# Window attention, software pipeline of one kernel: transposes three heads behind the scores, weightings on slots 0, 4, 8 and 12

## The chip, the cores and the metric

One Trainium2 chip, one core. The metric is the time of one execution on the device in microseconds; the value given is the median of three runs.

## The reference

Two blocks, each added to its input, on x of 2 x 128 x 128 x 128 (images, channels, rows, columns). The first is a group norm and window attention with relative position bias, the second a group norm and a deformable convolution. The change touches the first only:

```python
xw = x.reshape(B, C, H // ws, ws, W // ws, ws)            # ws = 16, 8 heads of 16 channels
xw = xw.transpose(0, 2, 4, 3, 5, 1).reshape(-1, N, C)     # 128 windows of N = 256 tokens
qkv = xw @ qkv_w.T + qkv_b
attn = jnp.einsum('whnd,whmd->whnm', q, k) * scale
attn = jax.nn.softmax(attn + bias[None], axis=-1)
out = jnp.einsum('whnm,whmd->whnd', attn, v)
out = out @ proj_w.T + proj_b
x = x + out
```

## The kernel before

Attention runs over 64 pairs of windows. A pair has 16 slots, one for each head of its two windows (slots 0 to 7 the first window, 8 to 15 the second). Every engine has its own program, written out by hand slot by slot in a function `pair` (L552 on TensorE, L637 on ScalarE, L749 on VectorE, L362 on SP), and the engines meet only through semaphores, so each engine works strictly in the order of its `pair`. Two pairs make the body of a loop. The first sixteen of the pairs in a loop also take the statistics of the second image on VectorE (L741).

The way of one head: TensorE makes its scores from `stack` into one of two buffers of `s_ps` (L508); they may be overwritten once VectorE is through with the head two before (L505). VectorE adds the bias and takes the row minimum (L716) into `sbias` and `nmax`. ScalarE takes the exponential into `prob` (L623), one of four buffers. TensorE transposes it in four pieces into one of three banks of `pt_ps` (L521); odd heads share one bank. The transposed head is copied to `probT`, even heads by ScalarE (L630), odd ones by VectorE (L725). When four heads are there, TensorE weights the values with them, without dividing (`weigh`, L536), into `o_ps`. The column of ones in `va` gives the row sums along with it. After two weightings, one window, ScalarE copies `o_ps` to `oT` (L635), TensorE transposes that into `x_ps` (`turn_out`, L548), VectorE divides into `on` (`norm`, L731 and L736), and SP stores it to `attended` (L359).

The lags are constants: T_LAG is how many slots after its scores a head is transposed, READ_LAG_A and READ_LAG_V the slot in which ScalarE and VectorE copy it, PV_LAG the slot in which `o_ps` is copied, OUT_AT that of `turn_out` (and the one after it `norm`). Each of these counts from the first head or half of the pair.

In the same slots the next pairs are prepared: TensorE projects q and k of the pair after next in slots 0 and 4 (L486, L490) and v of the next pair in slot 8 (L496), all into `qkv_ps`; ScalarE reads q in slot 1 (L611) and k in slot 4 (L616), VectorE reads v in slot 9 (L703). GpSimd normalises x and splits q and k into three bfloat16 parts (L443 to L452); SP stores these parts (`store_parts`, L340) and loads them again into `stack` as the terms of the score product (`restack`, L354, twelve transfers of 128 KB). All DMAs of attention are issued on SP's queue, in this order: clear a part of far_sums, load a strip of x, restack the next pair, store the second window of the pair before, store the parts, store the first window of this pair.

Of the kernel before, what the change touches and what calls it, by code (L numbers as in the profile page):

```python
# [20 lines left out]
NH = 8  # L21
# [3 lines left out]
PAIRS = B * (H // WS) * (W // WS) // 2  # L25
# [6 lines left out]
SCALE = float(HD) ** -0.5  # L32
T_LAG = 2
READ_LAG_A, READ_LAG_V = 3, 2
PV_LAG = 4
Q_AT, K_AT, V_AT = 0, 4, 8
OUT_AT = 6
AHEAD = 2
# [141 lines left out]
def attention(nc, x, w_qkv, b_qkv, bv_row, rel_rev, attended, rel_rows, parts_dram, info_out, far_sums):  # L180

    with ExitStack() as ctx:
# [15 lines left out]
        gmat = sb("a_gmat", [P, P])  # L199
# [5 lines left out]
        ex = sb("a_ex", [P, 2])  # L205
        gst = sb("a_gst", [P, 2])
# [93 lines left out]
        def _(sp):  # L300
# [61 lines left out]
            def pair(p, par, first=False, left=AHEAD, piece=None):  # L362
# [20 lines left out]
                if not first:  # L383
                    store(p - 1, 1, 1 - par)
                if left == AHEAD:
                    store_parts(p + 2, par)
                store(p, 0, par)

# [12 lines left out]
            pair(PAIRS - 1, 1, left=0)  # L401
            store(PAIRS - 1, 1, 1)
            for par in range(2):
# [66 lines left out]
        def _(pe):  # L470
# [4 lines left out]
            def group_sums(b):  # L475
                pe.wait_ge(gn_step, count(3 * b + 3))
                nc.tensor.matmul(x_ps[:, 0:2], gmat[:], ex[:], start=True, stop=True).then_inc(gn_sum, 1)
                pe.wait_ge(gn_coef, count(9 * b + 1))
# [73 lines left out]
            def pair(p, par, first=False, left=AHEAD):  # L552
                for n in range(SLOTS):
# [3 lines left out]
                    elif not first:  # L557
                        turn(p - 1, n - T_LAG + SLOTS)
                    if n % 4 == 3:
                        if n > 3:  # L560
                            weigh(p, (n - 7) // 4, par)
                        elif not first:
                            weigh(p - 1, 3, 1 - par)
                    if n == OUT_AT and not first:
# [26 lines left out]
            for n in range(SLOTS - T_LAG, SLOTS):  # L591
                turn(PAIRS - 1, n)
            weigh(PAIRS - 1, 3, 1)
            turn_out(2 * PAIRS - 1, 1)
# [79 lines left out]
        def _(dve):  # L674
            def scales(b):
# [5 lines left out]
                dve.wait_ge(gn_sum, count(b + 1))  # L681
                group_scales(nc, dve, x_ps[:, 0:2], gst, gv, gn[:, b, 0:1], gn[:, b, 1:2], gn_coef, 9 * b,
                             gn_ready, 2 * b, gn_root, b)
# [65 lines left out]
            def pair(p, par, first=False, left=AHEAD, piece=None):  # L749
                for n in range(SLOTS):  # L750
# [6 lines left out]
                    if n == OUT_AT + 1 and not first:  # L757
                        norm(2 * p - 1, 1, 1 - par, (p - 1) // 2)
                    if n == NH + OUT_AT + 1:
                        norm(2 * p, 0, par, p // 2)  # L760
                    if n == V_AT + 1 and left >= 1:
# [15 lines left out]
            for m in range(SLOTS - READ_LAG_V, SLOTS):  # L777
                if m % 2 == 1:
                    read_turned(PAIRS - 1, m)
            norm(2 * PAIRS - 1, 1, 1, (PAIRS - 1) // 2)  # L780

# [964 lines left out]
```

## Time and profile before

| | |
|---|---|
| time, median of 3 runs | 3287.48 us (3285.68 to 3289.9) |
| time of the profiled execution | 3290.47 us, span 3288.8 us |
| attention | some 84 to 1527 us of the span |
| busy over the whole span | TensorE 83%, VectorE 83%, ScalarE 56%, GpSimd 35% |
| one steady pair of windows | 22.35 us |

The span covers both blocks; the deformable convolution follows attention and shares no time with it. For a change in attention the shares over the whole span say little, so the rows below are of the steady stretch of attention, in which one pair is like the next. Matmuls are pipelined on TensorE and their ends are modelled, so steps are best read from start to start. A number in square brackets at the end of a timeline row is the time in which the engine stood idle before it, with the instruction that ended the wait.

### The profile page before, as it was taken

The page shows a single profiled execution, that of the slowest core. Times are in us where ns is not written, and L with a number is a line of the kernel's source. Part 1 is how long each engine was busy: PE and PEld are TensorE (multiplying, and loading weights), DVE is VectorE, ACT ScalarE, POOL GpSimd, SP SyncE. Part 2 cuts the span into 40 slices and gives each one's busy share as a digit, 9 for nine tenths or more (in the row PEclk, how much of TensorE's full clock was granted, in tenths as well). Part 3 has the DMA queues.
Part 4 walks back from the last instruction along what each step waited for, and adds up shares of the span by engine and source line. Part 5 has one row for each costly group of instructions (what it writes and reads, how often), then busy time and mean ns, then how long its engine had stood idle before and what let it go on. Part 6 is the DMA issues. An engine that isn't in the chain of part 4 may idle for free.

```text
span 3288.8 us, 77998 instructions
## 1 busy us (share of the span) xinstructions
PE 2733.5 (83%) x22424; PEld 2192.2 (67%) x22424; DVE 2719.8 (83%) x6553; ACT 1828.7 (56%) x3486; POOL 1162.0 (35%) x1557
## 2 busy tenths in 40 slices
PE   1888889999999999995677989998946799999986
PEld 0555555565565556564566888887835688888885
DVE  3888888888888888885667999999945799999996
ACT  0888888888888888884143443333202443334420
POOL 3333233333333333332446231346232441115550
PEclk9999999999999999998988999999978899999998
DMA  7889897888888898895553233333374433333334
GB/s 182 158 157 163 166 148 138 139 140 143 138 141 142 141 139 143 140 144 116 183 158 91 89 99 101 99 103 84 89 261 134 144 101 101 97 101 95 102 89 160
DMA packets 351779, 432.59 MB, mean 132 GB/s; under 512 B 42352, under 2 KB 275200, under 8 KB 346480
## 3 DMA queue, kind: packets, MB, share of 16 engines
q1 hardware_dynamic: 339696, 423.85, 58.5%
q0 software_dynamic: 11904, 6.44, 1.5%
q8 instruction: 102, 1.67, 0.2%
q14 instruction: 77, 0.63, 0.1%
HBM read 283.33 MB, written 147.09 MB: 131 GB/s over the span
## 4 chain that ended last, share of the span: by engine, by line
DVE 24%; issue 10%; DMA 6%; PE 5%; POOL 3%; DVEq 1%; ACT 1%; POOLq 1%; SPq 1%; ACTq 0%
DVE prod L1635 17%; DMA vring<-vals 3%; DVE tt L1619 2%; PE sum_ps L1429 2%; DVE my L1614 2%; DMA vring<-attended 1%; DVE x L1646 1%; PE sum_ps L1384 1%; ACT d_xn L1518 1%; DMA o_sel<-off_out,pos 1%; PE om_ps L1347 1%; POOL gath L1209 1%; PE sum_ps L1333 1%; POOLq L1216 1%; DMA out<-x 0%
## 5 line engine op out<-in xcount | busy, mean ns | idle before, releaser
L623 ACT ACTIVATE prob<-sbias,nmax 128x256 f32<-128x256 f32 x2048 | 903.9, 501 | 203.4 <-DVE nmax L716 201.0
L716 DVE CUSTOM_DVE_ANT_0 sbias<-s_ps,nbias 128x256 f32<-128x256 f32 x2048 | 768.0, 420 | 212.8 <-PE s_ps L508 201.4
L1635 DVE TENSOR_TENSOR prod<-vring,wt_ps 128x1920 f32<-128x1920 f32 (+3 forms) x512 | 898.8, 1815 | 18.8 <-DMA vring<-vals 11.9
L1384 PE MATMUL sum_ps<-d_ident,prod 128*128 128x128 f32 x6400 | 773.0, 279 | 83.5 <-DVE prod L1635 83.4
L1384 PEld LDWEIGHTS sum_ps<-d_ident,prod 128*128 128x128 f32 x6400 | 732.0, 144 | 131.8 <-DVE prod L1635 104.3
L521 PE MATMUL pt_ps<-a_ident,prob 128*128 128x128 f32 x4096 | 645.3, 280 | 140.5 <-ACT prob L623 137.5
L521 PEld LDWEIGHTS pt_ps<-a_ident,prob 128*128 128x128 f32 x4096 | 448.2, 141 | 284.3 <-DVE probT L725 134.3
L1484 ACT ACTIVATE hat<-off,one_col 128x576 f32<-128x576 f32 x128 | 140.7, 1099 | 700.6 <-DVE tt L1619 700.6
L508 PE MATMUL s_ps<-stack 96*128 96x256 bf16 x2048 | 396.6, 275 | 8.1 <-DMA stack<-parts_dram 7.4
L443 POOL CAST parts<-qk 128x1024 bf16<-128x1024 f32 x64 | 66.3, 1036 | 869.9 <-ACT qk L616 869.9
L725 DVE COPY probT<-pt_ps 128x512 f32<-128x512 f32 x512 | 351.9, 687 | 11.9 <-PE pt_ps L521 11.8
L1362 PE MATMUL wt_ps<-tt,d_ident 128*128 128x144 f32 x2304 | 311.1, 291 | 0.0
L508 PEld LDWEIGHTS s_ps<-stack 96*128 96x128 bf16 x2048 | 175.2, 98 | 202.5 <-issue 157.4
L1362 PEld LDWEIGHTS wt_ps<-tt,d_ident 128*128 128x128 f32 x2304 | 306.6, 195 | 1.4
L630 ACT COPY probT<-pt_ps 128x512 f32<-128x512 f32 x512 | 290.2, 567 | 0.0
L536 PE MATMUL o_ps<-probT,va 128*32 128x256 f32 x4096 | 274.1, 385 | 0.9 <-DVE probT L725 0.9
L1224 POOL COPY first_e<-first_at 128x2 f32 x16 | 2.9, 178 | 563.9 <-issue 563.9
L1619 DVE TENSOR_TENSOR tt<-hat,my 128x864 f32<-128x864 f32 x192 | 192.5, 1057 | 8.8
L716 DVE DVE_READ_ACCUMULATOR2_ANT nmax<- 128x1 f32 x2048 | 170.7, 83 | 0.0
L536 PEld LDWEIGHTS o_ps<-probT,va 128*32 128x32 f32 x4096 | 106.9, 109 | 87.9 <-issue 34.1
L1333 PE MATMUL sum_ps<-wproj_sb,vring 128*128 128x128 f32 x512 | 81.9, 321 | 90.4 <-DMA vring<-attended 81.3
L446 POOL TENSOR_TENSOR rest<-qk,parts 128x1024 f32<-128x1024 f32 x64 | 137.0, 2141 | 11.8 <-POOL parts L443 11.8
(170 smaller groups left out, 3382.2 us busy)
## 6 DMA issues: line engine op xcount, KB each, us to landing
stack<-parts_dram SPq DMA_DIRECT2D x768, 128.0 KB, 7.6
vring<-vals SPq DMA_DIRECT2D x270, 320.0 KB
parts_dram<-parts SPq DMA_DIRECT2D x64, 768.0 KB, 6.5
off_out<-off SPq DMA_DIRECT2D x64, 432.0 KB
strips<-x SPq DMA_DIRECT2D x68, 256.0 KB, 3.7
far_sums<-nothing SPq DMA_DIRECT2D x64, 256.0 KB, 2.1
attended<-on SPq DMA_DIRECT2D x256, 64.0 KB
x<-x SPq DMA_DIRECT2D x16, 1024.0 KB, 6.5
```

The costliest lines, as they stand in the source:

```text
L508: mm = nc.tensor.matmul(s_ps[:, n % 2, half, :], stack[:, par, 0, h, at:at + P], stack[:, par, 1, h, w * NT:(w + 1) * NT], start=True, sto ...
L521: mm = nc.tensor.transpose(pt_ps[:, T_BANK[n % 4], kh, half * P:(half + 1) * P], prob[:, n % 4, half, kh * P:(kh + 1) * P], ident[:])
L536: mm = nc.tensor.matmul(o_ps[32 * j:32 * j + VA, t * NT:(t + 1) * NT], va[:, par, 2 * w + kh, 4 * t + j, :], probT[:, (4 * k + j) % 8, kh, ...
L623: ins = nc.scalar.activation(prob[:, n % 4, half, :], sbias[:, n % SBIAS, half, :], ACT.Exp, bias=nmax[:, n % SBIAS, half:half + 1], scale ...
L630: nc.scalar.copy(probT[:, n % 8], pt_ps[:, T_BANK[n % 4]]).then_inc(t_read_a, 1)
L716: ins = nc.vector.tensor_tensor_reduce(out=sbias[:, n % SBIAS, half, :], in0=s_ps[:, n % 2, half, :], in1=nbias[:, h, half, :], scale=1.0, ...
L725: nc.vector.tensor_copy(probT[:, n % 8], pt_ps[:, T_BANK[n % 4]]).then_inc(t_read_v, 1)
L1362: mm = nc.tensor.matmul(acc[:, :, jx:jx + KS, jy * G:(jy + KS) * G], ident[:], tt[:, jx, jy, 2 * half:2 * half + 2].rearrange("p r (a k) - ...
L1384: mm = nc.tensor.matmul(sum_ps[:, par, r * H:(r + 1) * H], prod[:, r % 2, dx, dy * C:(dy + 1) * C], ident[:], start=(r + dx + dy == 0), st ...
L1484: nc.scalar.activation(xy(hat[:, j]), xy_off(s), ACT.Abs, bias=0.0 if j == 1 else one_col[:, j // 2:j // 2 + 1]).then_inc(dist_ready, 1)
L1619: ins = nc.vector.tensor_tensor(tt[:, jx], hat[:, jx, :, 0:KG].unsqueeze(1) .to_broadcast([P, 3, COLS, KG]), my[:], ALU.mult)
L1635: nc.vector.tensor_tensor(prod[:, r % 2, first:last].rearrange("p a (t c) -> p (a t) c", c=CG), vring[:, at:at + wide].rearrange("p a (t c ...
```

## The change

T_LAG goes from 2 to 3, and the copies of the transposed heads, the copy of o_ps and turn_out move one slot later with it. The weightings move from slots 3, 7, 11 and 15 to slots 4, 8, 12 and 0, so that the third weighting of a pair falls into slot 0 and the fourth into slot 4 of the next. The norm of a pair's first window falls into slot 0 of the next pair. SP stores both windows of the pair before behind the restacking and ahead of the parts. The sums of the group norm go to `qkv_ps` instead of `x_ps`. The projections and the readings of q, k and v stay where they are.

```diff
--- before.py
+++ after.py
@@ -30,11 +30,11 @@
 VA = 32
 SBIAS = 8
 SCALE = float(HD) ** -0.5
-T_LAG = 2
-READ_LAG_A, READ_LAG_V = 3, 2
-PV_LAG = 4
+T_LAG = 3
+READ_LAG_A, READ_LAG_V = 4, 3
+PV_LAG = 5
 Q_AT, K_AT, V_AT = 0, 4, 8
-OUT_AT = 6
+OUT_AT = 7
 AHEAD = 2
 GN_EPS = 1e-5
 CHUNK = 4 * W
@@ -381,10 +381,10 @@
                 if left >= 1:
                     restack(p + 1, 1 - par)
                 if not first:
-                    store(p - 1, 1, 1 - par)
+                    for w in range(2):
+                        store(p - 1, w, 1 - par)
                 if left == AHEAD:
                     store_parts(p + 2, par)
-                store(p, 0, par)
 
             store_parts(0, 0)
             restack(0, 0)
@@ -399,7 +399,8 @@
             pair(PAIRS - 3, 1)
             pair(PAIRS - 2, 0, left=1)
             pair(PAIRS - 1, 1, left=0)
-            store(PAIRS - 1, 1, 1)
+            for w in range(2):
+                store(PAIRS - 1, w, 1)
             for par in range(2):
                 sp.wait_ge(y_out[par], count(64 * (PAIRS // 2)))
             sp.wait_ge(far_cleared, count(16 * PAIRS))
@@ -474,7 +475,7 @@
 
             def group_sums(b):
                 pe.wait_ge(gn_step, count(3 * b + 3))
-                nc.tensor.matmul(x_ps[:, 0:2], gmat[:], ex[:], start=True, stop=True).then_inc(gn_sum, 1)
+                nc.tensor.matmul(qkv_ps[:, 0:2], gmat[:], ex[:], start=True, stop=True).then_inc(gn_sum, 1)
                 pe.wait_ge(gn_coef, count(9 * b + 1))
 
             group_sums(0)
@@ -556,11 +557,11 @@
                         turn(p, n - T_LAG)
                     elif not first:
                         turn(p - 1, n - T_LAG + SLOTS)
-                    if n % 4 == 3:
-                        if n > 3:
-                            weigh(p, (n - 7) // 4, par)
+                    if n % 4 == 0:
+                        if n >= 8:
+                            weigh(p, n // 4 - 2, par)
                         elif not first:
-                            weigh(p - 1, 3, 1 - par)
+                            weigh(p - 1, n // 4 + 2, 1 - par)
                     if n == OUT_AT and not first:
                         turn_out(2 * p - 1, 1)
                     if n == NH + OUT_AT:
@@ -590,7 +591,8 @@
             pair(PAIRS - 1, 1, left=0)
             for n in range(SLOTS - T_LAG, SLOTS):
                 turn(PAIRS - 1, n)
-            weigh(PAIRS - 1, 3, 1)
+            for k in (2, 3):
+                weigh(PAIRS - 1, k, 1)
             turn_out(2 * PAIRS - 1, 1)
 
         @block.scalar
@@ -679,7 +681,7 @@
                 nc.vector.scalar_tensor_tensor(out=ex[:, 1:2], in0=mv[:, 0:1], scalar=mv[:, 0:1], in1=mv[:, 1:2],
                                                op0=ALU.mult, op1=ALU.add).then_inc(gn_step, 1)
                 dve.wait_ge(gn_sum, count(b + 1))
-                group_scales(nc, dve, x_ps[:, 0:2], gst, gv, gn[:, b, 0:1], gn[:, b, 1:2], gn_coef, 9 * b,
+                group_scales(nc, dve, qkv_ps[:, 0:2], gst, gv, gn[:, b, 0:1], gn[:, b, 1:2], gn_coef, 9 * b,
                              gn_ready, 2 * b, gn_root, b)
 
             for n in range(NSTAT):
@@ -756,8 +758,8 @@
                         read_turned(p if m >= 0 else p - 1, m % SLOTS)
                     if n == OUT_AT + 1 and not first:
                         norm(2 * p - 1, 1, 1 - par, (p - 1) // 2)
-                    if n == NH + OUT_AT + 1:
-                        norm(2 * p, 0, par, p // 2)
+                    if n == 0 and not first:
+                        norm(2 * p - 2, 0, 1 - par, (p - 1) // 2)
                     if n == V_AT + 1 and left >= 1:
                         read_v(p + 1, 1 - par)
 
@@ -777,7 +779,8 @@
             for m in range(SLOTS - READ_LAG_V, SLOTS):
                 if m % 2 == 1:
                     read_turned(PAIRS - 1, m)
-            norm(2 * PAIRS - 1, 1, 1, (PAIRS - 1) // 2)
+            for w in range(2):
+                norm(2 * PAIRS - 2 + w, w, 1, (PAIRS - 1) // 2)
 
 
 def deformable(nc, x, attended, w_proj, bproj_row, w_value, bv_row, w_om, bom_row, w_out, b_out, vals, off_out, info_out, far_sums, out):
```

## Rows read from the trace of the kernel before

**Rows 1.** Stage table, steady pair: window, length, PE, PEld, DVE, ACT, POOL busy, clock, DMA
```profile
632.26:654.61 22.35, 20.26 (x185) 13.39 (x181) 18.48 (x81) 19.42 (x45) 7.80 (x7) 1.00 0.87 141
```

**Rows 2.** Table of waits, 700 to 1300 us: total us, times, longest
```profile
PE pt_ps L521 <- ACT prob L623: 54.9, 121, 0.6
```

**Rows 3.** Timeline of TensorE: start us, length, line, tiles; slots 3 to 3
```profile
614.52 1.07 PE L536 MATMUL o_ps<-probT,va 128*32 128x256 f32 x16
615.52 0.39 PE L508 MATMUL s_ps<-stack 96*128 96x256 bf16 x2
...
616.21 1.02 PE L490 MATMUL qkv_ps<-xn,wqkv_sb 128*128 128x512 f32 x2
617.07 0.38 PE L508 MATMUL s_ps<-stack 96*128 96x256 bf16 x2
...
617.73 0.38 PE L508 MATMUL s_ps<-stack 96*128 96x256 bf16 x2
...
618.44 0.65 PE L548 MATMUL x_ps<-a_ident,oT 128*128 128x128 f32 x4
...
619.81 0.65 PE L521 MATMUL pt_ps<-a_ident,prob 128*128 128x128 f32 x4 [0.49 <-ACT prob L623]
620.39 1.07 PE L536 MATMUL o_ps<-probT,va 128*32 128x256 f32 x16
...
622.06 1.06 PE L496 MATMUL qkv_ps<-wqkv_sb,xn 128*128 128x128 f32 x8
622.96 0.38 PE L508 MATMUL s_ps<-stack 96*128 96x256 bf16 x2
...
625.96 1.07 PE L536 MATMUL o_ps<-probT,va 128*32 128x256 f32 x16
...
631.26 1.07 PE L536 MATMUL o_ps<-probT,va 128*32 128x256 f32 x16
632.26 0.39 PE L508 MATMUL s_ps<-stack 96*128 96x256 bf16 x2
...
636.87 1.07 PE L536 MATMUL o_ps<-probT,va 128*32 128x256 f32 x16
```

**Rows 4.** Timeline of ScalarE in the same pair, slots 1 to 7
```profile
614.18 0.69 ACT L611 ACTIVATE qk<-qkv_ps,bqn_sb 128x512 f32<-128x512 f32 x1
...
616.92 0.91 ACT L623 ACTIVATE prob<-sbias,nmax 128x256 f32<-128x256 f32 x2
617.73 0.56 ACT L635 COPY oT<-o_ps 128x512 f32<-128x512 f32 x1
618.20 0.69 ACT L616 ACTIVATE qk<-qkv_ps,bqkv_sb 128x512 f32<-128x512 f32 x1
618.78 0.90 ACT L623 ACTIVATE prob<-sbias,nmax 128x256 f32<-128x256 f32 x2
619.58 0.57 ACT L630 COPY probT<-pt_ps 128x512 f32<-128x512 f32 x1
620.04 1.71 ACT L623 ACTIVATE prob<-sbias,nmax 128x256 f32<-128x256 f32 x4
```

**Rows 5.** Timeline of VectorE, slot 9 and the start of slot 10
```profile
623.53 0.43 DVE L716 CUSTOM_DVE_ANT_0 sbias<-s_ps,nbias 128x256 f32<-128x256 f32 x1 [0.72 <-PE s_ps L508]
...
624.22 0.69 DVE L725 COPY probT<-pt_ps 128x512 f32<-128x512 f32 x1
624.83 0.68 DVE L703 TENSOR_TENSOR va<-qkv_ps,bv_sb 128x512 f32<-128x512 f32 x1
625.42 0.41 DVE L716 CUSTOM_DVE_ANT_0 sbias<-s_ps,nbias 128x256 f32<-128x256 f32 x1
```

**Rows 6.** Timeline of SP's DMA issues in the same pair
```profile
615.16 5.54 SPq L354 DMA_DIRECT2D stack<-parts_dram  x12
...
626.27 0.35 SPq L340 DMA_DIRECT2D parts_dram<-parts  x1
```

**Rows 7.** Page, DMA issues: count, KB each, median us to landing
```profile
stack<-parts_dram SPq DMA_DIRECT2D x768, 128.0 KB, 7.6
```

## Prediction

> **What bounds the kernel now.** I read the stage table first, then the waits of the steady stretch, then three timelines (TensorE, ScalarE, VectorE) of one window pair. In a steady pair of 22.35 us no engine is full: PE is busy 20.26, ScalarE 19.42, VectorE 18.48, the DMA engines 0.87 [rows 1]. So a loop through several engines sets the pace, not one engine. The table of waits names one: over 600 us (27 pairs) PE sat 54.9 us before transposes (L521), waiting for exponentials [rows 2]. That is 2.0 us a pair, and it is the wait at which the change aims. The reader must go one step further and ask what else would have held PE there.
>
> I write "slot n" for the turn of head n (0 to 15), S(n) for its scores, E(n) for its exponential. PE issues in order, so whatever waits holds all behind it. A weighting W takes four heads; L528 and L529 make it wait until all four are copied to probT. Its last even head is copied by ScalarE in the queue behind an exponential two slots before W. So there is this loop: W, then scores, VectorE's bias and minimum, ScalarE's exponential, ScalarE's copy, next W. I walk it round one pair, in steps from start to start:
> - W to the scores behind it 1.00 (614.52 to 615.52); scores and transposes of one slot 0.66 (617.07 to 617.73); a projection 0.86 for q or k (616.21 to 617.07), 0.90 for v (622.06 to 622.96) [rows 3].
> - Scores to their exponential, if nothing is queued ahead: 1.40 (S(4) 615.52 to E(4) 616.92) [rows 3, 4].
> - ScalarE: an exponential holds the next work up 0.80 (two heads 1.71, one 0.91; 618.78 to 619.58), the copy of o_ps (L635) 0.47, the reading of k 0.58 [rows 4]; the reading of q has the same length, 0.69, and is priced the same.
> - Exponential to W: 618.78 to 620.39, 1.61 [rows 3, 4].
>
> From the W of slot 3 to that of slot 7: 1.00 to S(4), 1.40 to E(4), then 0.80, 0.47 and 0.58 on ScalarE to E(5), then 1.61: 5.86; measured 5.87. Slot 7 to 11: 1.00, slot 8's 0.66, v 0.90, 1.40, 1.61: 5.57; measured 5.57. Slot 11 to 15: 1.00, 1.40, 0.80, 0.47, 1.61: 5.28; measured 5.30. Slot 15 to 3: 1.00, 0.66, q 0.86, 1.40, 1.61: 5.53; measured 5.61 [rows 3]. Sum 22.24, measured 22.35. This loop is the bound, and it goes round just as well without the wait that the table names.
>
> **The change, part by part.**
>
> *Transposes and weightings one slot later.* No instruction is added or removed. T_LAG 3 sets the transposes of head n into slot n+3, READ_LAG_A and _V move the copies by one, and the weightings move from slots 3, 7, 11, 15 to 4, 8, 12, 0. The transposes gain a slot of slack against the exponential (even heads lose 0.6 of it, since the bank they reuse is now copied out only behind that exponential). But W moves together with its copy: the copy of head 4k+2 stood in slot 4k+5 before a W in slot 4k+7, and stands in 4k+6 before one in 4k+8. The lead is two slots, as before. So where a transpose stops waiting, W waits for the copy a fraction of a microsecond later, and scores, transposes, copies of x_ps and projections are queued behind it on PE; VectorE starves for the scores and ScalarE for VectorE.
>
> *What stands in the loop now.* The projections stay at slots 0, 4 and 8, and W falls on the same slots, so PE issues W and a projection back to back, 1.86 or 1.90, with no scores between. s_ps holds only two heads of scores, so behind this burst ScalarE is empty. Then two exponentials come in a row before the copy that W needs, with a reading between them; before the change the first of these two ran while PE did the projection. With c for copy to W:
> - W(slot 0) to W(slot 4): 1.00, q 0.86, S(1) to E(1) 1.40, 0.80, reading of q 0.58, E(2) 0.80, c: 5.44 + c.
> - Slot 4 to 8: 1.00, k 0.86, 1.40, 0.80, copy of o_ps 0.47 (now in slot 5), E(6) 0.80, c: 5.33 + c. The reading of k falls into the time before E(5).
> - Slot 8 to 12: 1.00, v 0.90, S(9) to E(10), 0.80, c. VectorE puts slot 9's minimum, 0.69, and the reading of v, 0.59, ahead of slot 10's [rows 5], so S(9) to E(10) is 1.40 + 1.28 = 2.68: 5.38 + c.
> - Slot 12 to 0: 1.00, 1.40, 0.80, copy of o_ps 0.47, 0.80, c: 4.47 + c.
>
> Sum 20.62 + 4c. The trace bounds c: the copy at 619.58 has its W at 620.39, 0.81, but that W starts 0.58 behind a transpose (619.81) that itself had waited, so c may be less; the copy of o_ps at 617.73, equally long, has its transposes at 618.44, 0.71 [rows 3, 4]. Nothing in these waits lets PE start before the copy ends 0.56 after its start, so no gain is hidden here. I take the middle, 0.76, as a W has more waits to pass than those transposes. The period is 23.66 us (23.46 to 23.86), **1.31 us more than 22.35** (1.11 to 1.51; up to 1.62 if the walk also misses 0.11, as it did above).
>
> *Norms.* One moves from slot 7 to 8, the other from 15 to the next slot 0. VectorE is waiting for PE's burst right behind both, so I cost them at nothing; without that cover each would put the next minimum back by its own length, which I bound by nothing and two copies of 0.69 [rows 5].
>
> *The SP queue.* The stores move past the clearing of far_sums, the strip load and the 12 restacking issues. Now SP waits for the norm of slot 15 before it may restack, and issues from 615.16 for 5.54 us, with 7.6 us to landing, so some 628.3 against the next pair's scores at 632.26 [rows 3, 6, 7]. After, restacking no longer waits for that norm and its store, only for the parts to land and the scores that read the old stack, so it comes earlier. The two stores follow it, the second behind slot 8's norm, and store_parts behind them. Splitting ends for store_parts in the second half of the pair (626.27 now), about when that norm is done. The gain has no taker and the delay no victim: the buffers of stores are wanted again two pairs later. Nothing either way.
>
> *Group sums in qkv_ps instead of x_ps.* The same instructions once per image, needed because x_ps is now read a slot later. Nothing. At the end one weighting and one transpose leave the last pair for the tail: within 1 us.
>
> **The sum.** Pairs 1 to 61 have all three bursts: 61 x 1.31 = 80 us; pair 62 has one, 0.5. The first sixteen also carry statistics on VectorE; I give them the same increment. Against the profiled execution, 3290.5 us (span 3288.8), that is 3371; it lies 3 us above the median of the runs, 3287.5, and so I forecast **3368 us**, 2.4% slower. For c at its ends, and with 0.11 on top: 61 x 1.11 = 68 to 61 x 1.62 = 99, so 3355 to 3387.
>
> **The rivals.**
> 1. *The transposes' wait is the bound, as the table says.* With one slot more of slack PE loses its 2.0 us a pair: 62 x 2.0 = 124, so 3163 us, PE's 20.26 being the new pace. For it: the wait is real and on the fullest engine. Against it: it would need a W that is free of the copy two slots before, and both walks go through that copy. It decides if copy to W were hidden, that is if the two exponentials behind a burst took under 0.3 us together instead of 1.6. A smaller gain lies between. Chance 6%.
> The Trainium skill, "Perfetto Trace Analysis", section "Optimization Strategy", says that the same gap repeating on the engine that should be saturated can mean too few buffers for the next tile. The gap repeats here, and more lag is what that rule would prescribe; by it the time is rival 1's. The two walks speak against it: the gap is filled by the next wait in the same loop.
> 2. *The bursts cost nothing net.* Without what is queued on ScalarE and VectorE the loop has the same sum before and after: 1.00, slot 0.66, the projections, 1.40 and 1.61. If the readings found room elsewhere, the pair would stay at 22.35 and the time within 0.2% of 3287. Against it: both queues are in program order, and the readings stand in the listed slots. Also here: the lag and the bursts cancel. Chance 4%.
> 3. *More is lost than the walk has.* Transposes of odd heads share one bank, so they also wait for VectorE's copy; turn_out in slots 7 and 15 waits for the copy of o_ps. In the walk both end before W's own wait, the second only just: E(5), 0.80, 0.71, then turn_out, scores and transposes, some 1.15, make 2.66, against 0.80, 0.47, 0.80 and 0.76, that is 2.83, for the W of slot 8. If that copy or VectorE's came one copy's length, 0.5 us, later, 0.3 would stick out at each of the two places: 61 x 0.6 = 37 more, 3405. Chance 10%.
> Forecast: 80%.
>
> **How the numbers follow.** About 0.2% (7 us) is what a measurement of this kernel can tell from no change. Faster by more than that 0.06, within it 0.04, slower 0.90, from the cases above. The range runs from 3345 to 3395: the sum's bounds, with 10 us below for steps read from one pair only and 8 above towards rival 3. It leaves out rivals 1 and 2 and most of 3.
>
> **What would show it.** Right: steady pairs of about 23.7 us; the wait of L521 for the exponential almost gone and a wait of L536 for L630 in its place, mostly in slots 4 and 12; the gaps between W starts near 6.2, 6.1, 6.1 and 5.2; VectorE idle longer before L716 for scores, after slots 0, 4 and 8; restacking issued some us earlier, with no one starting sooner. Wrong: pairs under 22.3 us with PE free of waits at L536 (rival 1), or pairs near 22.35 in which the readings lie in idle time (rival 2); PE waits at L548 or for VectorE's copies that add up to more than W's (rival 3).

## The result and the profile after

The changed kernel takes 3372.72 us (median; 3367.92 to 3376.22) against 3286.84 us of the kernel before beside it: a ratio of 1.0259, 95% interval 1.0241 to 1.0277. It is 2.6% slower. Forecast were 3368 us, 80 us more than before; measured are 86 more. The profiled execution of after took 3369.52 us, its span 3367.8.

In the code of after the lines stand a little lower: the weighting W is L537, the transposes L522, the scores L509, turn_out L549, the projections L487, L491 and L497, the exponential L625, ScalarE's copies L632 (to probT) and L637 (of o_ps), VectorE's minimum L718 and its copy L727.

First the stage table of one steady pair, from a W in slot 4 to the next one, as [rows 1] (columns: stretch, its length, then busy time of PE, weight loads, VectorE, ScalarE, GpSimd, each with its instructions, granted clock, DMA share, GB/s):

```profile
909.10:932.84 23.74, 20.49 (x180) 13.67 (x180) 18.25 (x80) 19.49 (x45) 7.81 (x7) 1.00 0.85 135
```

Each engine does the work of [rows 1] in the same busy time within 0.3 us, but the pair takes 23.74 us for 22.35. Two pairs, the body of the loop, alternate between 23.59 and 23.75, 23.67 in the mean. The 1.32 us a pair over the 46 steady pairs are 61; the first sixteen, with the statistics on VectorE, went from 22.79 to 24.28 and add 24. So practically the whole of the 86 us is time in which the same work waits, spread over all pairs.

Then the waits in the same 600 us as [rows 2] (engine, line waited for, us in total, times, longest):

```profile
DVE sbias L718 <- PE s_ps L509: 130.9, 152, 2.2
ACT prob L625 <- DVE nmax L718: 101.3, 128, 1.4
...
PEld o_ps L537 <- ACT probT L632: 44.9, 89, 1.2
...
PE x_ps L549 <- ACT oT L637: 33.7, 51, 0.7
...
PE o_ps L537 <- ACT probT L632: 23.4, 29, 0.9
```

and the first two of them in the kernel before:

```profile
DVE sbias L716 <- PE s_ps L508: 85.2, 134, 0.8
ACT prob L623 <- DVE nmax L716: 78.1, 121, 1.1
```

The wait that led the list of PE before, transposes for the exponential [rows 2], is no longer listed. In its place PE and its weight loads wait at W for the copy, PE waits at turn_out for the copy of o_ps, and VectorE and ScalarE wait much longer for their input, 130.9 for 85.2 us and 101.3 for 78.1.

PE in one pair, to be laid beside [rows 3] (start, length, engine, line, operation; in brackets the idle time before and what ended it):

```profile
902.86 1.07 PE L537 MATMUL o_ps<-probT,va 128*32 128x256 f32 x16
903.86 1.12 PE L487 MATMUL qkv_ps<-xn,wqkv_sb 128*128 128x512 f32 x2
904.82 0.38 PE L509 MATMUL s_ps<-stack 96*128 96x256 bf16 x2
...
909.10 1.07 PE L537 MATMUL o_ps<-probT,va 128*32 128x256 f32 x16 [0.91 <-ACT probT L632]
910.10 1.12 PE L491 MATMUL qkv_ps<-xn,wqkv_sb 128*128 128x512 f32 x2
911.06 0.38 PE L509 MATMUL s_ps<-stack 96*128 96x256 bf16 x2
...
913.96 0.65 PE L549 MATMUL x_ps<-a_ident,oT 128*128 128x128 f32 x4 [0.67 <-ACT oT L637]
...
914.67 0.60 PE L522 MATMUL pt_ps<-a_ident,prob 128*128 128x128 f32 x4
915.21 1.07 PE L537 MATMUL o_ps<-probT,va 128*32 128x256 f32 x16
916.21 1.16 PE L497 MATMUL qkv_ps<-wqkv_sb,xn 128*128 128x128 f32 x8
917.20 0.38 PE L509 MATMUL s_ps<-stack 96*128 96x256 bf16 x2
...
921.30 1.07 PE L537 MATMUL o_ps<-probT,va 128*32 128x256 f32 x16
...
925.21 0.65 PE L549 MATMUL x_ps<-a_ident,oT 128*128 128x128 f32 x4 [0.66 <-ACT oT L637]
...
926.04 0.65 PE L522 MATMUL pt_ps<-a_ident,prob 128*128 128x128 f32 x4
926.62 1.07 PE L537 MATMUL o_ps<-probT,va 128*32 128x256 f32 x16
```

W and a projection stand back to back three times in a pair, and 1.96 to 1.99 us pass from a W to the next scores. I call W and a projection back to back a burst. What it does to VectorE, behind slot 4, and then ScalarE in the same pair (the same columns; two views):

```profile
911.63 0.42 DVE L718 CUSTOM_DVE_ANT_0 sbias<-s_ps,nbias 128x256 f32<-128x256 f32 x1 [2.19 <-PE s_ps L509]
```

```profile
906.29 0.91 ACT L625 ACTIVATE prob<-sbias,nmax 128x256 f32<-128x256 f32 x2 [1.34 <-DVE nmax L718]
907.11 0.67 ACT L613 ACTIVATE qk<-qkv_ps,bqn_sb 128x512 f32<-128x512 f32 x1
907.68 0.90 ACT L625 ACTIVATE prob<-sbias,nmax 128x256 f32<-128x256 f32 x2
908.48 0.57 ACT L632 COPY probT<-pt_ps 128x512 f32<-128x512 f32 x1
...
912.44 0.91 ACT L625 ACTIVATE prob<-sbias,nmax 128x256 f32<-128x256 f32 x2 [0.49 <-DVE nmax L718]
913.26 0.56 ACT L637 COPY oT<-o_ps 128x512 f32<-128x512 f32 x1
913.73 0.91 ACT L625 ACTIVATE prob<-sbias,nmax 128x256 f32<-128x256 f32 x2
914.53 0.57 ACT L632 COPY probT<-pt_ps 128x512 f32<-128x512 f32 x1
...
919.87 0.91 ACT L625 ACTIVATE prob<-sbias,nmax 128x256 f32<-128x256 f32 x2 [0.38 <-DVE nmax L718]
920.69 0.56 ACT L632 COPY probT<-pt_ps 128x512 f32<-128x512 f32 x1
...
923.70 0.91 ACT L625 ACTIVATE prob<-sbias,nmax 128x256 f32<-128x256 f32 x2 [0.37 <-DVE nmax L718]
924.52 0.56 ACT L637 COPY oT<-o_ps 128x512 f32<-128x512 f32 x1
924.98 0.91 ACT L625 ACTIVATE prob<-sbias,nmax 128x256 f32<-128x256 f32 x2
925.79 0.57 ACT L632 COPY probT<-pt_ps 128x512 f32<-128x512 f32 x1
```

VectorE stands idle 2.19 us until the scores behind the burst are there. Then ScalarE has an exponential, a copy of o_ps and a second exponential to do before it comes to the copy at 914.53, which W at 915.21 needs.

### The profile page after: what moved, and what is told of

It is laid out like the page before. It is cut to its first block, busy times and chain, and to the rows that moved or that the text cites. A ratio compares the mean times of both kernels' runs of the same rounds, so it can differ in the third digit from the quotient of the medians.

```text
span 3367.8 us, 78088 instructions
## 1 busy us (share of the span) xinstructions
PE 2741.8 (81%) x22424; PEld 2210.4 (66%) x22424; DVE 2703.9 (80%) x6553; ACT 1835.2 (54%) x3486; POOL 1161.0 (34%) x1557
## 4 chain that ended last, share of the span: by engine, by line
DVE 23%; issue 10%; DMA 7%; PE 5%; POOL 3%; DVEq 1%; ACT 1%; POOLq 1%; SPq 1%; ACTq 0%
DVE prod L1638 17%; DMA vring<-vals 3%; DVE tt L1622 2%; DMA vring<-attended 2%; PE sum_ps L1432 2%; DVE my L1617 1%; DVE x L1649 1%; DMA o_sel<-off_out,pos 1%; PE sum_ps L1387 1%; PE sum_ps L1336 1%; ACT d_xn L1521 1%; PE om_ps L1350 1%; POOL gath L1212 1%; DMA out<-x 0%; POOLq L1219 0%
## 5 line engine op out<-in xcount | busy, mean ns | idle before, releaser
L625 ACT ACTIVATE prob<-sbias,nmax 128x256 f32<-128x256 f32 x2048 | 909.9, 501 | 274.4 <-DVE nmax L718 271.3
L718 DVE CUSTOM_DVE_ANT_0 sbias<-s_ps,nbias 128x256 f32<-128x256 f32 x2048 | 758.8, 420 | 327.0 <-PE s_ps L509 326.7
L522 PE MATMUL pt_ps<-a_ident,prob 128*128 128x128 f32 x4096 | 626.4, 275 | 37.4 <-DVE probT L727 37.0
L522 PEld LDWEIGHTS pt_ps<-a_ident,prob 128*128 128x128 f32 x4096 | 472.8, 141 | 91.4 <-DVE probT L727 71.6
L509 PE MATMUL s_ps<-stack 96*128 96x256 bf16 x2048 | 398.0, 276 | 39.5 <-DVE nmax L718 29.8
L727 DVE COPY probT<-pt_ps 128x512 f32<-128x512 f32 x512 | 351.0, 686 | 1.6 <-PE pt_ps L522 1.6
L537 PE MATMUL o_ps<-probT,va 128*32 128x256 f32 x4096 | 274.7, 386 | 63.0 <-ACT probT L632 58.2
L509 PEld LDWEIGHTS s_ps<-stack 96*128 96x128 bf16 x2048 | 162.0, 98 | 214.6 <-DVE nmax L718 102.3
L632 ACT COPY probT<-pt_ps 128x512 f32<-128x512 f32 x512 | 289.4, 565 | 0.0
L537 PEld LDWEIGHTS o_ps<-probT,va 128*32 128x32 f32 x4096 | 107.1, 109 | 158.2 <-ACT probT L632 106.0
L718 DVE DVE_READ_ACCUMULATOR2_ANT nmax<- 128x1 f32 x2048 | 170.2, 83 | 0.0
L549 PE MATMUL x_ps<-a_ident,oT 128*128 128x128 f32 x512 | 83.5, 286 | 84.0 <-ACT oT L637 84.0
```

Source lines behind the costliest of these rows:

```text
L509: mm = nc.tensor.matmul(s_ps[:, n % 2, half, :], stack[:, par, 0, h, at:at + P], stack[:, par, 1, h, w * NT:(w + 1) * NT], start=True, sto ...
L522: mm = nc.tensor.transpose(pt_ps[:, T_BANK[n % 4], kh, half * P:(half + 1) * P], prob[:, n % 4, half, kh * P:(kh + 1) * P], ident[:])
L537: mm = nc.tensor.matmul(o_ps[32 * j:32 * j + VA, t * NT:(t + 1) * NT], va[:, par, 2 * w + kh, 4 * t + j, :], probT[:, (4 * k + j) % 8, kh, ...
L625: ins = nc.scalar.activation(prob[:, n % 4, half, :], sbias[:, n % SBIAS, half, :], ACT.Exp, bias=nmax[:, n % SBIAS, half:half + 1], scale ...
L632: nc.scalar.copy(probT[:, n % 8], pt_ps[:, T_BANK[n % 4]]).then_inc(t_read_a, 1)
L718: ins = nc.vector.tensor_tensor_reduce(out=sbias[:, n % SBIAS, half, :], in0=s_ps[:, n % 2, half, :], in1=nbias[:, h, half, :], scale=1.0, ...
```

## The experiments

Three causes were weighed: the burst, the lead (W comes only two slots behind a copy that stands behind two exponentials), and SP's order. Most kernels change constants alone: READ_LAG_A, the slot of ScalarE's copy to probT; PV_LAG, that of its copy of o_ps; Q_AT, K_AT and V_AT, those of the projections. "Pair" is the period of W, the mean from 700 us to 1250, with the four gaps (slots 0, 4, 8 and 12 to the next W; where W stands in slots 3, 7, 11 and 15, from 15 on). The runs come from several sessions, in which the kernel before took 3286 to 3292 us; each ratio is to the kernel before of its own session, and a difference between rows of two sessions is good to some 5 us.

| kernel | us | ratio to before (95%) | pair, us (gaps) |
|---|---|---|---|
| before | 3287 | 1 | 22.35 (5.61, 5.87, 5.57, 5.30) |
| after | 3372.72 | 1.0259 (1.0241 to 1.0277) | 23.67 (6.23, 6.11, 6.10, 5.23) |
| stores_old | 3380.15 | 1.0278 (1.0259 to 1.0298) | 23.67 (6.23, 6.11, 6.10, 5.23) |
| copy_early | 3373.33 | 1.0259 (1.0240 to 1.0279) | 23.57 (5.25, 6.73, 5.88, 5.72) |
| o_early | 3306.61 | 1.0051 (1.0028 to 1.0075) | 22.59 (6.23, 5.58, 6.10, 4.68) |
| copy_o_early | 3215.68 | 0.9774 (0.9750 to 0.9798) | 21.01 (5.25, 5.58, 5.88, 4.30) |
| proj_apart | 3178.65 | 0.9670 (0.9653 to 0.9688) | 20.41 (5.07, 5.27, 4.85, 5.23) |
| apart_o | 3143.41 | 0.9545 (0.9526 to 0.9564) | 19.94 (4.70, 5.31, 4.73, 5.20) |
| apart_o_copy | 3099.63 | 0.9417 (0.9402 to 0.9433) | 19.18 (4.72, 5.09, 4.78, 4.59) |
| turn_alone | 3307.38 | 1.0049 (1.0028 to 1.0069) | 22.42 (5.54, 5.78, 5.95, 5.15) |
| turn_apart | 3254.62 | 0.9887 (0.9871 to 0.9904) | 21.67 (5.23, 6.13, 5.16, 5.15) |
| before_proj_apart | 3348.28 | 1.0168 (1.0149 to 1.0186) | 23.38 (6.00, 6.19, 5.79, 5.41) |
| before_copy_early | 3361.51 | 1.0221 (1.0201 to 1.0242) | 23.47 (5.76, 6.35, 5.57, 5.78) |
| weigh_late | 3559.57 | 1.0830 (1.0801 to 1.0859) | 26.8; undisturbed 26.1 (6.83, 6.66, 6.82, 5.84) |

**SP's order.** After, with the store of a first window put back to its old place, ahead of the clearing, the strip and the restacking:

```diff
             def pair(p, par, first=False, left=AHEAD, piece=None):
+                if not first:
+                    store(p - 1, 0, 1 - par)
...
                 if not first:
-                    for w in range(2):
-                        store(p - 1, w, 1 - par)
+                    store(p - 1, 1, 1 - par)
```

> The changed kernel with the order of SP's stores put back: the store of a pair's first window goes ahead of the next pair's clearing, strip load and restacking, as in the kernel before. Theory A: SP is off the loop, so 3372 us within 7. Theory C, that stores behind the restacking cost time: part of the 86 us comes back, below 3350.

No gain. It is 7 us more, a microsecond outside my range, with intervals that overlap those of after, and the gaps are those of after to 0.01 us. SP is not in the loop. Its queue in after, beside [rows 6]:

```profile
900.56 5.54 SPq L354 DMA_DIRECT2D stack<-parts_dram  x12
```

Restacking begins 1.5 us before the scores of slot 0 (902.11) instead of 5.2 us behind them, and nobody starts the sooner for it.

**The projections away from W.** After, with the projections two slots later:

```diff
-Q_AT, K_AT, V_AT = 0, 4, 8
+Q_AT, K_AT, V_AT = 2, 6, 10
```

> The changed kernel with the projections moved off the weightings' slots (Q_AT, K_AT, V_AT 2, 6, 10 instead of 0, 4, 8); the readings move with them. Lags and copies as changed. Theory A: a projection behind the scores of slot s+2 is no longer between a weighting and the exponential that its successor needs; with copy to weighting 0.62 us (as measured in the changed kernel) the four passes are 4.6, 5.1, 4.6 and 5.1 us, 19.4 in all, below ScalarE's own work, so some other limit of 19.5 to 21.5 us a pair takes over: 3372 - 61 x (2.2 to 4.2) = 3116 to 3238 us. Theory B (bursts alone) expects a gain here too, back to about the kernel before, 3287, or a little below. Theory C: 3372.

As expected: 194 us less than after and 3.3% less than before. The four W keep their slots and their lead over the copy; the bursts are gone. But the readings of q, k and v move along with the projections, and the walk had those of q and v in two of its gaps. From slot 4 to 8, where it had none, the gap fell by 0.84; from 0 to 4 and from 8 to 12, where it had one, by 1.16 and 1.25. So most of the gain is the bursts', and a smaller part may be the readings'; no run parts the two. What is left of the waits:

```profile
DVE sbias L718 <- PE s_ps L509: 56.4, 89, 0.8
```

130.9 us in after, with single waits of up to 2.2 us, are now 56.4 with none over 0.8.

**The copy earlier.** After, with ScalarE's copy to probT a slot sooner, so that W has three slots behind it:

```diff
-READ_LAG_A, READ_LAG_V = 4, 3
+READ_LAG_A, READ_LAG_V = 3, 3
```

> The changed kernel with one constant put back: READ_LAG_A 3 instead of 4, so ScalarE copies an even head one slot earlier and a weighting stands three slots behind its copy instead of two. The bursts (weighting and projection back to back in slots 0, 4, 8) stay. Theory A, the loop runs through weighting, scores, two exponentials, copy, weighting: one exponential (0.8 us) and the reading beside it (0.5 us) fall out of each of the four passes, so that weighting no longer waits; the next limits are about 20 to 22 us a pair, so 3372 - 61 x (1.7 to 3.7) = 3147 to 3268 us, clearly below the kernel before. Theory B, the burst on TensorE alone starves VectorE and ScalarE, whatever the copy does: the pair stays at 23.7 us and the time within 20 us of 3372. Theory C, the SP queue with its stores behind the restacking is late: no change either, 3372.

A miss: 3373.33, the time of after. W's wait for L632 has left the table, and the gap from slot 0 to 4 fell by 1.0 us, but the next gap rose by 0.6 and the last by 0.5. The time is the one that theories B and C named; stores_old speaks against C, and copy_o_early below against B. The waits of copy_early show where it went (33.7 in after):

```profile
PE x_ps L549 <- ACT oT L637: 61.8, 51, 1.3
```

and its two timelines of PE and ScalarE show why:

```profile
909.88 0.57 ACT L632 COPY probT<-pt_ps 128x512 f32<-128x512 f32 x1
910.35 0.59 ACT L637 COPY oT<-o_ps 128x512 f32<-128x512 f32 x1
```

```profile
911.08 0.65 PE L549 MATMUL x_ps<-a_ident,oT 128*128 128x128 f32 x4 [1.28 <-ACT oT L637]
```

The copy for W now stands ahead of the copy of o_ps in the same slot of ScalarE's queue, and turn_out, which has PE's queue behind it, waits 1.28 us for the latter. This is the wait of the prediction's third rival.

**The copy of o_ps earlier, and both.** To part the two waits, o_early moves only the copy of o_ps (PV_LAG 5 to 4), and copy_o_early both copies.

> The changed kernel with PV_LAG 4 instead of 5: ScalarE copies o_ps in slots 4 and 12, where the changed kernel's ScalarE stands idle behind the burst, instead of between the two exponentials of slots 5 and 6 (13 and 14) on which the next weighting waits. Nothing else moves. Theory A (the loop, with all that stands on ScalarE's queue between burst and copy): 0.47 us fall out of two of the four passes, and turn_out no longer waits for that copy: 0.5 and 0.6 to 0.7 us, so 1.0 to 1.2 us a pair, 3372 - 61 to 73 = 3299 to 3311 us. Theory B (the burst alone starves the others): no change, 3372 within 10. Rival 3 of the prediction (turn_out's wait is the larger part) expects the whole of its wait back, more than 1.3 us a pair, below 3293.

> The changed kernel with both copies of ScalarE earlier: READ_LAG_A 3 and PV_LAG 4. In the run with READ_LAG_A 3 alone the weighting no longer waited, but turn_out in slots 7 and 15 did, as the copy of o_ps now stood behind the other copy: one tied wait had taken the place of another. Theory A: with both out of the way the next limits are the odd heads' bank and VectorE, some 5.3 us for each of three passes and 4.4 for the fourth, 20.3 us a pair, at most 21.5: 3372 - 61 x (2.2 to 3.4) = 3165 to 3238 us, though the bursts stay. Theory B (burst alone): 3372 within 20.

Both as expected. o_early shortens the gaps that held turn_out by 0.53 and 0.54 and leaves the others; that is 66 us. Both together are worth 157, where the one is worth 66 and the other nothing: two waits were tied, and the wait for the copy of o_ps hid what the copy to probT cost. In copy_o_early all three bursts are still there, and it is 2.3% faster than before. So the burst alone is not the cause either; it costs because two copies stand late in the queue that runs dry behind it.

**The same two moves on the kernel before.**

> The kernel before with READ_LAG_A 2 instead of 3: a weighting then stands three slots behind ScalarE's copy, with nothing else changed. In the kernel before the transposes wait for the exponential at the same time as the weighting waits for the copy. Theory A with that tie: one of the two waits taken away alone brings nothing, as the transposes still hold TensorE: the pair stays within 0.4 us of 22.35, so 3287 us within 25. If weighting had been the only bound of the kernel before, the pair would fall to about 21 us or less and the time to 3200 or below. Rival 1 of the prediction (the transposes' wait alone was the bound) also expects no change here.

> The kernel before with only the projections moved, Q_AT, K_AT, V_AT 2, 6, 10, so two and three slots behind a weighting instead of one. Theory A: they leave the way from a weighting to the exponential that the next one needs; the passes are 4.7, 5.3, 4.7 and 5.3 us, 19.9 a pair, with some tenths for what else waits: 3287 - 61 x (1.5 to 2.4) = 3141 to 3196 us. If the lags of the change were what made the changed kernel with its projections apart fast (3179 us), the gain here would be smaller than half of that, above 3233. If the projections only cost where they meet a weighting in the same slot, nothing is gained here: 3287.

Both missed, and on the side that I had not allowed for: 2.2% and 1.7% slower. ScalarE of before_copy_early:

```profile
712.92 0.56 ACT L630 COPY probT<-pt_ps 128x512 f32<-128x512 f32 x1
713.38 0.59 ACT L635 COPY oT<-o_ps 128x512 f32<-128x512 f32 x1
713.86 0.70 ACT L616 ACTIVATE qk<-qkv_ps,bqkv_sb 128x512 f32<-128x512 f32 x1
714.44 1.70 ACT L623 ACTIVATE prob<-sbias,nmax 128x256 f32<-128x256 f32 x4
```

Three copies and readings in a row, 1.52 us, now stand in slot 4 ahead of head 5's exponential, which is itself in the loop; before, there were two, 0.47 and 0.58 [rows 4]. The gaps from slot 3 and slot 11 grew by that copy, 0.48 each. In before_proj_apart it is PE that is blocked:

```profile
912.36 0.65 PE L521 MATMUL pt_ps<-a_ident,prob 128*128 128x128 f32 x4 [0.70 <-ACT prob L623]
912.85 1.02 PE L486 MATMUL qkv_ps<-xn,wqkv_sb 128*128 128x512 f32 x2
```

With a lag of two, the projection's new slot puts it behind transposes that wait for an exponential; in its old slot it ran while that exponential was under way. The same constants that gave after 194 us cost before 56.

**The parts of the change alone.** turn_alone is the kernel before with T_LAG 3 and READ_LAG 3, 3, so that transposes and VectorE's copies come a slot later and W stays. weigh_late is after with T_LAG 2 and READ_LAG 3, 2: W comes a slot later, alone.

> One part of the change alone on the kernel before: T_LAG 3 and READ_LAG_A, READ_LAG_V 3, 3, everything else as before, so weightings stay in slots 3, 7, 11 and 15, apart from the projections, and ScalarE's copy stays two slots ahead of the weighting. Theory A: the transposes stop waiting for the exponential, and the weighting then waits for the copy, which frees it 0.2 us sooner than the transposes did: the passes are 5.7, 5.4, 5.1 and 5.3 us, 21.5 a pair; 3287 - 61 x 0.87 = 3234 us, between 3220 and 3287. Rival 1 of the prediction (the transposes' wait is the bound): 3163 or near it.

> The other part alone: the changed kernel with T_LAG 2 and READ_LAG_A, READ_LAG_V 3, 2 as before, so only the weightings (with what follows them) are a slot later and fall together with the projections; ScalarE's copy is three slots ahead of the weighting. Theory A: transposes of head s-2 stand right ahead of the weighting of slot s and wait for an exponential that comes two behind the burst, with a copy and a reading between: passes of 6.8, 6.7, 6.3 and 5.8 us, 25.6 a pair: 3372 + 61 x 1.9 = 3490 us, between 3430 and 3510. Theory B (the burst alone, the lag of the transposes without effect): 3372 within 20. If the weighting's wait for the copy were all that matters, three slots of lead would bring it below 3287.

turn_alone is the direct test of rival 1: the wait that led the table of before is taken away, and with it a gain of up to 124 us should come. It takes 3307.38 us, 0.5% more than before. It is not a clean test, though: VectorE's copies come a slot later and W does not, so their lead over W falls from two slots to one. Its waits:

```profile
PEld o_ps L536 <- ACT probT L630: 83.8, 108, 1.4
...
PE o_ps L536 <- DVE probT L725: 31.0, 27, 1.1
```

The wait is gone and another has its place. That is 20 us above my range, in which I had ScalarE's copies in the walk and not VectorE's: its copy of slot 10 stands behind the reading of v, and the W of slot 11 waits 1.1 us for it in each of 27 pairs; the gap from slot 7 to 11 is 5.95 for 5.57. Without these 0.38 us a pair, some 24 us, it would be about where before is, still far from 3163 (an estimate from the gaps). The other three gaps are 0.08 to 0.15 shorter than in before, and steady pairs of 22.42 us are all but those of before; of the 16 us more, some 11 lie in the first sixteen pairs, which take 23.46 us for 22.79. This I have only read from the trace, not tried.

weigh_late goes the expected way, 50 us further than the range. W has its lead, but the transposes wait for exponentials again (89.5 us in the same 600). Its undisturbed pairs take 26.1 us: (26.1 - 22.35) x 62 gives 233, some 3520 us. The rest has another cause (stages of 5 us, then PE):

```profile
946.00:951.00 5.00, 3.94 (x30) 2.29 (x22) 3.65 (x16) 3.12 (x8) 0.00 (x0) 1.00 1.19 122
951.00:956.00 5.00, 4.46 (x26) 2.25 (x27) 0.92 (x5) 2.71 (x8) 0.00 (x0) 0.66 1.17 115
```

```profile
949.76 0.65 PE L522 MATMUL pt_ps<-a_ident,prob 128*128 128x128 f32 x4 [0.70 <-ACT prob L625]
950.25 0.38 PE L509 MATMUL s_ps<-stack 96*128 96x256 bf16 x2
951.54 1.12 PE L522 MATMUL pt_ps<-a_ident,prob 128*128 128x128 f32 x4 [0.90 <-ACT prob L625]
952.58 1.94 PE L537 MATMUL o_ps<-probT,va 128*32 128x256 f32 x16
```

**The lag of three with projections apart.** turn_apart is turn_alone with the projections in slots 2, 6 and 10.

> Transposes three slots behind the scores (T_LAG 3, READ_LAG_A and _V 3, 3), weightings in the slots of the kernel before, and projections at 2, 6, 10. Theory A: with the projections off the loop, the lag alone is again worth little, since the weighting waits for the copies as long as the transposes did for the exponential: within 30 us of the kernel before with its projections apart, so 3140 to 3220 us. If the transposes' wait is the bound once the projections are away, this is at least 40 us below that run.

The first expectation failed by both of its numbers: the run is 94 us below before_proj_apart, where 30 at most were allowed, and 35 above the range of 3140 to 3220. The second, at least 40 below that run, came true. Once the projections are away, the transposes' wait for the exponential is a bound: PE's 64.6 us of it in before_proj_apart are off the list in turn_apart. Without the projections' shift the lag of three is worth nothing (turn_alone), without the lag the shift costs 56; together they are 1.1% faster than before. proj_apart, which has the weightings and what follows them a slot later as well, is another 76 us below it.

**The best of it.** apart_o is proj_apart with PV_LAG 4, apart_o_copy has READ_LAG_A 3 as well.

> The changed kernel with projections at 2, 6, 10 and the copy of o_ps in slots 4 and 12 (PV_LAG 4). In the run with the projections alone moved, turn_out still waited 0.65 us a pair in slot 15 and the copy stood between two exponentials of slots 5 and 13. Theory A: 0.6 to 0.8 us a pair less than 20.4: 3179 - 61 x 0.7 = 3136 us, between 3125 and 3150. If ScalarE's own work (some 18.9 us a pair) with its unavoidable starts is already the limit, 3179 within 10.

> The same with READ_LAG_A 3 as well, so that the weighting stands three slots behind ScalarE's copy. Theory A: the weighting's last wait, 0.34 us in slot 4, goes too: 19.3 to 19.6 us a pair, 3105 to 3135 us, near ScalarE's own work of 18.9. If the order of ScalarE's queue only moves the wait to turn_out or the transposes, as with this lag on the changed kernel, it is no faster than the run with the copy of o_ps alone early.

The first as expected, the second 5 us better than its range: 3099.63 us, 5.8% faster than before and 8.1% than after. Its stage row over 600 us and its first wait on PE:

```profile
700.00:1300.00 600.00, 595.98 (x5623) 428.72 (x5622) 565.84 (x2469) 588.12 (x1375) 242.18 (x218) 1.00 0.98 164
```

```profile
PE s_ps L509 <- DMA stack<-parts_dram: 2.8, 4, 1.7
```

PE is busy 99% of the stretch (with ends that are modelled), ScalarE 98%: next to no idle time is left on either. The first wait of PE on the list is for a restacking DMA. copy_early brought nothing on after; the same edit brings 44 us here.

## Why the prediction was right

**The bound of before.** I held that a loop through W, scores, exponential and copy sets the pace, and that the wait named by the table [rows 2] is only the place where it shows. turn_alone bears it out in the main: that wait taken away, the time is 0.5% up and not down to the 3163 us of rival 1. The loop does not go round "just as well", however. In before, W at 620.39 stands 0.81 behind its copy because the late transposes hold it [rows 3, 4]; in after a W that only its copy holds stands 0.61 or 0.62 behind it. So the transposes held that W some 0.2 us longer than its copy alone would have (an estimate from these rows), and three gaps of turn_alone are in fact shorter, by 0.08 to 0.15. The Trainium skill, "Perfetto Trace Analysis", section "Optimization Strategy", says that a gap that keeps repeating can mean too few buffers; here more slack at the gap alone gave no time, and no run added a buffer. With the projections moved as well, the slack was worth 94 us, so it is a condition of a gain.

**The walk of after.** The steps as forecast, and as measured between 902.86 and 926.62:

| from W to W | forecast | measured | of this, measured steps |
|---|---|---|---|
| slot 0 to 4 | 6.20 | 6.24 | 1.00, projection 0.96, S to E 1.47, 0.82, reading 0.57, 0.80, c 0.62 |
| 4 to 8 | 6.09 | 6.11 | 1.00, 0.96, 1.38, 0.82, copy of o_ps 0.47, 0.80, copy to W 0.68 |
| 8 to 12 | 6.14 | 6.09 | 1.00, 0.99, S(9) to E(10) 2.67, 0.82, c 0.61 |
| 12 to 0 | 5.23 | 5.32 | 1.01, 1.39, 0.82, 0.46, 0.81, copy to W 0.83 |
| pair | 23.66 | 23.76 | |

The order of the steps held in all four, except that in slots 8 and 0 something else let W go last (below). This pair is the longer of the two that alternate; their mean is 23.67.

**Two terms were mis-sized, and cancelled.** The first is c, copy to W. I took 0.76, between 0.71 and 0.81; where nothing else holds W it is 0.61 and 0.62, below the lower bound. My bounds were two rows of another kind: the 0.81 of a W behind late transposes, which I had noted, and the 0.71 of turn_out behind the copy of o_ps, which I took for the floor. turn_out takes as long in after, where it waits for nothing but that copy (0.70, from 913.26 to 913.96), so a W simply follows its copy sooner than turn_out does, although I had argued the contrary. The second is the burst: I priced a projection behind W at its price behind transposes, 0.86 and 0.90, and it was 0.96 and 0.99. That is +0.29 a pair against about -0.30 for c over the four places; the small steps add 0.1 in this longer pair. The fit to 0.01 us is thus in part luck; a step was good to about 0.1.

**In slots 8 and 0 the other path was as long, or longer.** There W does not follow its copy alone. In slot 0 the W at 926.62 stands 0.83 behind its copy but 0.58 behind the transposes of its slot, which stand behind scores and turn_out, which waited for the copy of o_ps; in slot 8 the W at 915.21 stands 0.68 behind its copy and 0.54 behind its transposes. Rival 3 priced this path 0.17 us short of W's own (2.66 against 2.83). If W's own path ends 0.62 behind its copy, as where nothing else holds it, then the other was longer by 0.06 in slot 8 and by 0.21 in slot 0 of this pair. The c that I had taken too large covered most of this, so it did little harm to the time. It did harm to what I expected next: copy_early removed one of two tied waits.

**What else was promised.** The wait of L521 for the exponential is gone, as said. The one at W came, but PE's own almost only in slot 4 (25 of 29 times, 22.8 of 23.4 us); in the others weight loads wait (44.9 us) or turn_out does. VectorE's idle time behind the bursts came: 2.19 us behind slot 4. Restacking came earlier, without a taker, and stores_old shows no cost of SP's order. The forecast was low by 5 us in all, about 3 of them in the first sixteen pairs, which lost 1.5 us each instead of the 1.31 that I gave them. The norms and the group sums had no experiment of their own; the walk leaves 0.1 us a pair or less for the norms.

**Why the loss, then.** Two things together: bursts of W and projection, behind which ScalarE is dry, and on ScalarE's queue two copies that come late behind exponentials. Take either away and the kernel is faster than before (3179 without the bursts, with the readings moved too; 3216 with the copies earlier). The expectations that failed by much (copy_early, before_copy_early, before_proj_apart, turn_alone) failed in one manner: I followed the wait that I removed, and not the others in the same two queues that the move pushed back. The Trainium skill, "Perfetto Trace Analysis", section "Per-engine timelines", calls the queues of ScalarE and VectorE strictly first in, first out; copy_early agrees for ScalarE, where the copy of o_ps begins at 910.35, 0.47 behind the one that was moved ahead of it.

## What to carry to other kernels

A wait that leads the table may be only the place where a loop through several in-order queues shows; walk the loop in steps from start to start, and after each edit walk it again through every queue that the moved instruction enters. When an edit takes a wait away and the time stays, look for a second wait that was tied with it, and move both before giving the edit up. Give a moved step a slot in which nothing else long stands, since two long steps back to back leave the engines behind them dry: here VectorE stood idle for 2.19 us.

## What the runs showed of the hardware

TensorE's clock fell to its lower level (1.2 of 2.4 GHz) for short stretches of weigh_late: the granted clock is 1.00 from 946 to 951 and 0.66 in the mean over 951 to 956. The waits of PE just before were only 0.70 and 0.90 us long, with transposes and scores in between. In copy_early, with waits of up to 1.28 us on PE, the granted clock was 1.00 over the 600 us, so the length of one wait doesn't decide it. The Trainium skill, "TensorE: Matmul & The Clock Gate", Part 1, says that "the default state is throttled, and activity releases the throttle"; that the clock fell in the kernel with the idlest PE (491 of 600 us busy, against 517 in after and 544 in before) agrees, without showing which part of it counted. What exactly made it fall in some pairs and not in others stays open.

The DMA engines ran at a mean share of 0.98 and 164 GB/s beside a PE that was busy 99%, against 0.87 and 140 in before, and PE's waits for them were 2.8 us in 600. A share of 0.98 is no ceiling here: over the 5 us from 946 in weigh_late it was 1.19. I had not expected that so much traffic would still land in time.
